# An attention and mixture-of-experts layer on one core: scores in four parts of the TensorE array, queries stored in groups of four tokens

## The reference

```python
q = concat([(cq @ Wcq + bcq).reshape(b, s, H, DH), rope((cq @ Wqr + bqr).reshape(b, s, H, DRH))], -1)
k = concat([(ckv @ Wck + bck).reshape(b, s, H, DH), rope((h_t @ Wkr + bkr).reshape(b, s, H, DRH))], -1)
v = (ckv @ Wv + bv).reshape(b, s, H, DH)
scores = einsum('bsid,bsjd->bsij', q, k) * SCALER      # per token: 16 x 16 over the heads
out = einsum('bsij,bsjd->bsid', softmax(scores), v).reshape(b, s, 512)
return out @ Wo + bo
```

## Time and profile before

| | us |
|---|---|
| median of 3 runs | 2026.46 (2020.72 to 2035.89) |
| the profiled execution | 2029.77 |
| its span, first to last instruction | 2027.8 |
| PE busy in the span | 1893.7 (93%) |
| DVE busy | 1520.7 (75%) |
| ACT busy | 1091.5 (54%) |
| POOL busy | 550.1 (27%) |
| 16 DMA engines, the share of queue q1 (issued by SP) | 53.1% |

### The profile page before, as it was taken

The page is one execution under the profiler, slowest core; times in us unless marked ns, Lnnn a source line. Parts: engine busy times, 40 slices in busy tenths (PEclk is TensorE's granted clock), DMA queues, the critical chain, the costliest instruction groups (busy, mean ns, idle before and its releaser), DMA issues. The chain is left out here.

```text
span 2027.8 us, 49115 instructions
## 1 busy us (share of the span) xinstructions
PE 1893.7 (93%) x14529; PEld 1504.8 (74%) x14529; DVE 1520.7 (75%) x3935; ACT 1091.5 (54%) x1745; POOL 550.1 (27%) x773
## 2 busy tenths in 40 slices
PE   5899999999999999999999999985899999988886
PEld 4788888888888888888888888874454555546664
DVE  6588888888888888888888888773444444429997
ACT  4576767666666767666666767651222233223333
POOL 1111112111111112111111111110344444427776
PEclk8799999999999999999999999997899999999998
DMA  5245454545454454545455554437999999979994
GB/s 189 69 129 147 128 153 129 151 128 150 124 143 138 133 150 128 150 129 152 126 140 137 137 146 128 140 108 222 334 299 284 274 310 307 291 202 394 406 398 171
DMA packets 414103, 383.99 MB, mean 189 GB/s; under 512 B 289704, under 2 KB 298024, under 8 KB 413992
## 3 DMA queue, kind: packets, MB, share of 16 engines
q1 hardware_dynamic: 393504, 324.98, 53.1%
q0 software_dynamic: 14336, 35.66, 7.5%
q10 hardware_dynamic: 6208, 22.68, 2.9%
HBM read 232.46 MB, written 150.63 MB: 189 GB/s over the span
## 5 line engine op out<-in xcount | busy, mean ns | idle before, releaser
L861 POOL TENSOR_SCALAR ve<-mv 128x1 f32<-128x1 f32 x192 | 42.7, 222 | 1073.1 <-DVE mv L698 1072.3
L593 ACT COPY qT<-bank 48x512 f32<-48x512 f32 x256 | 269.1, 1051 | 72.2 <-PE bank L445 67.6
L593 ACT COPY kT<-bank 48x512 f32<-48x512 f32 x256 | 268.8, 1050 | 4.8
L1068 PE MATMUL e_gu<-w,xgT 128*128 128x384 f32 x512 | 184.3, 503 | 15.4 <-DMA w<-w_ed 13.5
L452 PE MATMUL bank<-wgu,xfT 128*128 128x416 f32 x512 | 189.1, 369 | 8.3 <-ACT xfT L593 8.3
L453 PE MATMUL bank<-wgu,xfT 128*128 128x416 f32 x512 | 183.5, 358 | 0.0
L642 ACT ACTIVATE prob<-prob 128x512 f32<-128x512 f32 x128 | 78.7, 633 | 176.3 <-DVE prob L795 176.3
L469 PEld LDWEIGHTS score_ps<-kT,qT 48*64 48x64 f32 x4096 | 133.4, 138 | 40.7 <-issue 40.7
L469 PE MATMUL score_ps<-kT,qT 48*64 48x64 f32 x4096 | 151.1, 225 | 11.5 <-ACT kT L593 11.5
L1068 PEld LDWEIGHTS e_gu<-w,xgT 128*128 128x128 f32 x512 | 93.2, 192 | 74.7 <-DMA w<-w_ed 14.2
L1229 DVE SCALAR_TENSOR_TENSOR tanh<-tanh,e_gu 128x192 f32<-128x192 f32 x64 | 22.7, 354 | 166.3 <-ACT tanh L1155 166.3
(11 more groups left out here) (177 smaller groups left out, 4922.8 us busy)
## 6 DMA issues: line engine op xcount, KB each, us to landing
w<-w_eg SPq DMA_DIRECT2D x60, 768.0 KB, 6.7
acc_scratch<-zero SPq DMA_DIRECT2D x130, 256.0 KB, 4.2
w<-w_ed SPq DMA_DIRECT2D x60, 384.0 KB, 11.0
xf_scratch<-xf SPq DMA_DIRECT2D x64, 288.0 KB, 2.1
xin<-x SPq DMA_DIRECT2D x64, 256.0 KB, 2.9
v_scratch<-v SPq DMA_DIRECT2D x64, 256.0 KB, 3.7
vbd<-v_scratch SPq DMA_DIRECT2D x128, 128.0 KB, 3.2
o_scratch<-o SPq DMA_DIRECT2D x256, 64.0 KB, 2.3
```

The costliest lines, as they stand in the source:

```text
L593: nc.scalar.copy(dst, src).then_inc(done.sem, 1)
L1068: last = nc.tensor.matmul(gu_ps[par], xgT[:, par, n, :], w1[:, place, n, :], start=(n == 0), stop=(n == KD - 1))
```

## The change

- The contraction has 48 rows, so two blocks fit on top of one another in the array's 128 rows. `qT` and `kT` now use 128 partitions: tokens 0 to 63 of the tile stand in partitions 0 to 47, tokens 64 to 127 in 64 to 111. A block has a row part r as well as a column part g, and the matmuls go through the four pairs (g, r) in turn. The row part also chooses the bank of `score_ps`.
- The columns of a block of `qT` go by head and then token, where they went by token and then head: the four tokens of a head are now next to each other. `kT` keeps its order by token. So a row of the scores, and a partition of `o`, is (head, token).
- Each copy of `spread` becomes two, one for each half of the tokens, of 256 elements: eight for q and eight for k in a tile. Those of k write 16 elements apart as before; those of q write runs of four elements.
- All scores are issued in one stretch, with one increment, ahead of the transposes of `oin`; the wait for the rank copy of the tile before comes ahead of them. DVE's first maximum waits for all of them.
- The mask follows the new order of the rows. `o` is written to DRAM in four DMAs as before, with the same 128-byte runs. It is read back in four DMAs, one for each token of a group, each into every fourth partition of `oin` and in runs of 32 elements (128 bytes), where one DMA read rows of 2 KB. Two nops (`settle`) stand ahead of them on SP.

The diff at its core:

```diff
-    c[:, C_NEG:C_NEG + B4] = np.where((p[:, None] // H) % B4 == np.arange(B4), 0.0, -BIG)
+    c[:, C_NEG:C_NEG + B4] = np.where(p[:, None] % B4 == np.arange(B4), 0.0, -BIG)
...
-        qT, kT = qT_all[0:DQ], kT_all[0:DQ]
+        qT = qT_all[:, 0:P // 2, :].rearrange("p (c x) y -> p c (x y)", x=B4).rearrange("p c (h t) -> p c h t", t=B4)
+        kT = kT_all[:, 0:P // 2, :]
...
-                    dst = o_d[1 - par].rearrange("(c g b t) (h d) -> g b (t h) c d", c=8, g=2, b=2, h=H)
+                    dst = o_d[1 - par].rearrange("(c g b) (x d) -> g b x c d", c=8, g=2, b=2, d=DH)
...
                     sp.wait_ge(o_out.sem, o_out.at(i - 3))
+                    settle(sp)
                     sp.wait_ge(pe_oT.sem, pe_oT.at(i - 4))
-                    sp.dma_start(oin[:], o_d[1 - par]).then_inc(o_in.sem, 16)
+                    settle(sp)
+                    src = o_d[1 - par].rearrange("c (h t d) -> t c h d", t=B4, d=DH)
+                    for n in range(B4):
+                        sp.dma_start(oin[n:P:B4, :].rearrange("p (h d) -> p h d", d=DH), src[n]).then_inc(o_in.sem, 16)
...
-            def scores(blocks):
+            def scores():
-                for blk in blocks:
-                    for g in range(2):
-                        t0 = (blk // 2) * 16 + g * 8 + (blk % 2) * B4
-                        last = nc.tensor.matmul(score_ps[64 * g:64 * g + 64, blk * 64:blk * 64 + 64],
-                                                qT[:, t0:t0 + B4, :].rearrange("p t h -> p (t h)"),
-                                                kT[:, t0:t0 + B4, :].rearrange("p t h -> p (t h)"),
+                for blk in range(NBLK // 2):
+                    four = (blk // 2) * 4 + blk % 2
+                    for g, r in ((0, 0), (1, 1), (1, 0), (0, 1)):
+                        c4 = four + 2 * g
+                        part = slice(64 * r, 64 * r + DQ)
+                        at = r * 512 + blk * 64
+                        last = nc.tensor.matmul(score_ps[64 * g:64 * g + 64, at:at + 64],
+                                                qT[part, c4].rearrange("p h t -> p (h t)"),
+                                                kT[part, B4 * c4:B4 * c4 + B4, :].rearrange("p t h -> p (t h)"),
...
                     pe.wait_ge(a_pT.sem, a_pT.at(i - 3))
+                    pe.wait_ge(a_rank.sem, a_rank.at(i - 6))
                     settle(pe)
-                    scores(range(0, NBLK // 2)).then_inc(pe_s.sem, 1)
+                    scores().then_inc(pe_s.sem, 1)
                 if active(i - 3):
                     pe.wait_ge(o_in.sem, o_in.at(i - 3))
-                    pe.wait_ge(a_kT.sem, a_kT.at(i - 2, 2))
+                    pe.wait_ge(a_kT.sem, a_kT.at(i - 2, 4))
                     transposes(b3, [oin[:, n * P:(n + 1) * P] for n in range(KD)], pe_oT)
-                if active(i - 2):
-                    pe.wait_ge(a_rank.sem, a_rank.at(i - 6))
-                    settle(pe)
-                    scores(range(NBLK // 2, NBLK)).then_inc(pe_s.sem, 1)
...
-                    dv = dst.rearrange("p t (m a) -> p a m t", a=2)
                     for a in range(2):
-                        copy(dv[:, a, 4 * n:4 * n + 4, :],
-                             src[64 * a:64 * a + DQ, :].rearrange("p (m t) -> p m t", t=P), done)
+                        sv = src[64 * a:64 * a + DQ, :].rearrange("p (m r c t) -> p r m c t", m=4, r=2, t=B4)
+                        for r in range(2):
+                            copy(dst[64 * r:64 * r + DQ, a, 4 * n:4 * n + 4], sv[:, r], done)
...
-                    spread(qT, b3, a_qT, 0)
+                    by_four = qT.rearrange("p c (m a) t -> p a m c t", a=2)
+                    spread(by_four, b3, a_qT, 0)
...
-                    spread(kT, b3, a_kT, 0)
+                    by_token = kT.rearrange("p (c t) (m a) -> p a m c t", t=B4, a=2)
+                    spread(by_token, b3, a_kT, 0)
...
-                    dve.wait_ge(pe_s.sem, pe_s.at(i - 2, 1))
+                    dve.wait_ge(pe_s.sem, pe_s.at(i - 2))
...
-                    dve.wait_ge(pe_s.sem, pe_s.at(i - 2, 2))
```

More of the change, by code:

```diff
@@ L112, in layer_kernel @@
     v_d = nc.dram_tensor("v_scratch", (2, P, D), F32).ap()
-    o_d = nc.dram_tensor("o_scratch", (2, P, D), F32).ap()
+    o_d = nc.dram_tensor("o_scratch", (2, P // B4, B4 * D), F32).ap()
     rank_d = nc.dram_tensor("rank_scratch", (NT, E, P), BF16).ap()
@@ L260, in token_pipeline @@
         o_out = count("o_out", 64)
-        o_in = count("o_in", 16)
+        o_in = count("o_in", 64)
         x1_out = count("x1_out", 16)
@@ L275, in token_pipeline @@
         pe_kT = count("pe_kT", 2)
-        pe_s = count("pe_s", 2)
+        pe_s = count("pe_s")
         pe_pT = count("pe_pT", 2)
@@ L286, in token_pipeline @@
         a_latT = count("a_latT")
-        a_qT = count("a_qT", 4)
-        a_kT = count("a_kT", 4)
+        a_qT = count("a_qT", 8)
+        a_kT = count("a_kT", 8)
         a_exp = count("a_exp", 2)
@@ L499, in iteration @@
                     pe.wait_ge(d_lat.sem, d_lat.at(i - 2))
-                    pe.wait_ge(a_qT.sem, a_qT.at(i - 2, 2))
+                    pe.wait_ge(a_qT.sem, a_qT.at(i - 2, 4))
                     turn(k[:, par], pe_kT, 0, b3)
@@ L559, in iteration @@
                     pe.wait_ge(d_ln[0].sem, d_ln[0].at(i + 1))
-                    pe.wait_ge(a_kT.sem, a_kT.at(i - 2, 4))
+                    pe.wait_ge(a_kT.sem, a_kT.at(i - 2))
                     transposes(b2, [xn[:, n * P:(n + 1) * P] for n in range(KD)], pe_xT)
@@ L612, in iteration @@
                     act.wait_ge(pe_qT.sem, pe_qT.at(i - 2, 1))
-                    spread(qT, b3, a_qT, 0)
+                    by_four = qT.rearrange("p c (m a) t -> p a m c t", a=2)
+                    spread(by_four, b3, a_qT, 0)
                     act.wait_ge(pe_qT.sem, pe_qT.at(i - 2, 2))
-                    spread(qT, b7, a_qT, 1)
+                    spread(by_four, b7, a_qT, 1)
                 if active(i - 5):
@@ L621, in iteration @@
                     act.wait_ge(pe_kT.sem, pe_kT.at(i - 2, 1))
-                    spread(kT, b3, a_kT, 0)
+                    by_token = kT.rearrange("p (c t) (m a) -> p a m c t", t=B4, a=2)
+                    spread(by_token, b3, a_kT, 0)
                     act.wait_ge(pe_kT.sem, pe_kT.at(i - 2, 2))
-                    spread(kT, b2, a_kT, 1)
+                    spread(by_token, b2, a_kT, 1)
                 if active(i - 5):
```

## The result

| | before | after |
|---|---|---|
| median, us | 2027.97 (2020.72 to 2035.89, 4 runs) | 2133.5 (2129.88 to 2136.76, 4 runs) |
| ratio | | 1.0517, 95% interval 1.0486 to 1.0548 |
| the profiled execution, its span | 2029.77, 2027.8 | 2136.76, 2134.8 |
| PE busy | 1893.7 | 1870.7 (88%) |

What follows compares the result with a forecast made beforehand. PE bound the kernel at 20.66 us a tile; late reads would make the ring of o decide, adding 1.1 us for about 62 tiles, 68 us: 2095 us, 3.4% slower, range 2026 to 2136.

Steps and rivals of the forecast that it cites:

- the ring of o: DVE low part to o, SP write and read, PE transposes, ACT copy, next low part; 20.04 us, rising to 21.8.
- Issue of the four reads: SP's price to issue each rearranged read of o: 0.66 us, low end 0.34.
- Landing of the last read: Read of o on SP: a read lands 2.5 us after issue, the last at 629.43, 1.19 us late for PE's transposes.
- upper end of 3.2: Longest landing allowed for a read of o, from vbd's; with 0.66 an issue, 1.8 us a tile late.
- The clock stays where it is: PE's granted clock in the token stage was taken to stay at 1.00, the upper level (2.4 GHz).
- forecast ring: The ring of o after the change: 20.66 + 1.1 = 21.8 us a tile.
- the nops: Two nops on SP ahead of the reads of o, estimated at 0.05 us.
- DVE's own lateness: Leg from PE's transposes to DVE's next low part: 1.44 us, less up to 0.1 that DVE was itself late.
- The scores priced at nothing: PE's scores in one stretch of 1.08 to 2.16 us; the saving turns into waiting for the loads, priced at nothing.
- Rival (b): The packing pays: loads in time with 0.5 us to spare, PE loses 0.5 us a tile, 1995 us; chance 0.12.
- The copies: ACT's copies of 256 elements: q 0.373 us each, k 0.605; cost nothing, k ending where it did.
- SP's displaced queue: SP's DMAs behind the reads go out 2.3 us later, covered by 5 us of waiting for xf; nothing reaches an engine.

Runs made afterwards that it cites:

- One plain read: The changed kernel with its four reads of o replaced by one DMA of 2 KB rows, order of tokens left out; 1987.93 us, 0.9768 of before.
- the experiment on the read alone: The kernel before with only SP's new write addresses of o and four-DMA read behind two nops; 2230.35 us, 1.0978 of before.
- the two runs with head runs: Heads laid out so copies write runs of four words: changed kernel, q by token, one plain read, 1984.46 us; kernel before, scores unpacked, 2013.95 us.
- the run with both maxima first: The changed kernel with DVE taking the second half's score maximum before the low part of oT instead of behind it; 2093.78 us, 1.0334 of before.

## Why the prediction was right, and where its size was off

- **The bound: right.** The forecast had the ring of o take over from PE through the four reads. One plain read gives 1987.93, and shortening DVE's leg of the ring by one maximum gives 0.63 us a tile back, 0.48 of it in that leg. PE's wait alone does not decide: with the q products in it, the tile is still 22.21.
- **Issue of the four reads: right.** 0.66 was taken from the earlier trace rows; the median is 0.630, and 0.602 with runs of 512 bytes.
- **Landing of the last read: too low, the mis-sized term.** 2.5 was taken, as nearest to o_scratch's 2.3 in size. From its issue to the transposes the last read takes 2.90 us in the mean of the inner tiles (4.85 less the 1.95 of three issues), and 2.37 to 3.84 in single ones. For one read 2.5 was right: it is the median of the same four reads in the experiment on the read alone. But PE waits for the last of four, and the last of four is not a typical one: in that run it lands in 2.89 in the mean, up to 4.9. In runs of 512 bytes the stretch from its issue to the transposes is 2.33 and hardly varies. So this term is short by 0.4 us a tile. The prediction's upper end of 3.2, from vbd, covers it.
- **"The clock stays where it is": wrong, and small.** It is 0.95. A slow Wo product makes y late (0.37 us of DVE's idle time in the tile shown), and y stands ahead of o on DVE, so it enters the ring: low part to end of o is 12.00 us from 631.00 (the next o starts at 642.31) where it was 11.57. That tile is among the longest; in the mean of the inner tiles the leg is 11.63. With PE's wait filled the clock is 1.00 and the tile 0.22 shorter, which the times of the two runs do not tell from nothing. With PE waiting amid the scores this term is large (13.23 in the mean of the experiment on the read alone).
- **Together:** forecast ring 21.76, in the inner tiles 22.33, so 0.57 is missing. Landing gives 0.40 of it, DVE's leg 0.06 and the nops 0.05 (they cost 0.10 and not 0.05: from the last write's landing to the first read it is 0.12 us with them, also in the run with one plain read, and 0.02 without). The last 0.1 is what the prediction took off behind the transposes, as DVE's own lateness: that leg is 1.43, as it was. The issues, 1.95 for 1.98, gave 0.03 back. So 2133.5 us stands 38 above the forecast's 2095 and only just inside its range.
- **The scores priced at nothing: right.** PE's scores fell from two stretches of 1.15 to one of 1.16, and the saving turned into a longer wait (1.98 us). With a read that is in time it does pay: 20.67 to 20.14 us a tile and 2013.95 to 1984.46 us, packing as the main difference between the two runs with head runs (the single stretch of scores and the doubled number of copies come with it). Rival (b) had 1995 for it.
- **The copies: right.** q at 0.367 (taken 0.373), k at 0.602 (taken 0.605). The rule on lines of 16 bytes that the prediction named from the Trainium skill (SBUF — State Buffer, section Door 1: The DMA port swizzle) agrees with both, though it speaks of full rate and not of engines' prices.
- **SP's displaced queue: right.** SP still waits 287.3 us for xf, against 335.4; no engine waits for what was moved.

## What to carry to other kernels

Before changing a layout to make compute cheaper, follow the ring that the data runs in, through every queue: here a layout that saved about 1.1 us of matmuls and 1.2 us of q's copies a tile put some 2.1 us into a read (4.85 for 2.70) on a ring with 0.6 to spare. Put the permutation where its stride is free, on the reading side of a copy out of a bank, and keep DMAs in long runs. Where a step waits for several transfers, price the last of them to land and not a typical one: here a median of 2.5 us stood for a last one of 2.9.

## What the hardware showed that was not expected

- A rearranged read costs SP 0.63 us an issue with runs of 128 bytes and still 0.60 with runs of 512; four plain reads of the same 64 KB go out in 1.73, 0.43 each, and the one of 256 KB in 0.34.
- A copy that reads its bank 512 bytes apart and writes runs of 16 bytes takes 367 ns, as much as one that reads contiguously; writing single words 64 bytes apart takes 602.
- 64 matmuls of 48 x 64 in four parts of the array take 1.16 us, where 32 in two column parts took 1.15: two row parts work fully side by side.
- Four reads in runs of 128 bytes land in a median of 2.5 us, but the fourth of them in 2.89 in the mean and up to 4.9; in runs of 512 bytes the wait behind the fourth issue is 2.23 to 2.55 in the inner tiles.
- The length of PE's wait does not tell whether the products behind it run slow. In the changed kernel a wait of 1.98 us was followed by Wo products of 0.63, and the next one, of 2.30, by 0.43 and 0.40. In the run with both maxima first they took 0.63 behind 2.08 us, and 0.47 and then 0.39 behind 1.31; with the read alone a wait of 1.52 was followed by slow products and one of 1.44 not. How far a stall costs more than itself is to be read from the products behind it.
